# Feed-forward of two layers: the last 42 values and 42 gates share one column tile of the first matrix

## What is computed

```python
HID = int(DIM * 4 * 2 / 3)              # 682
h = shift_token(x)
mu, var = h.mean(-1, keepdims=True), h.var(-1, keepdims=True)
h = (h - mu) / jnp.sqrt(var + 1e-05) * lg + lb
h = h @ w1 + b1                         # w1: 256 x (2 * 682)
a, g = jnp.split(h, 2, axis=-1)         # values, gates
h = a * jax.nn.gelu(g, approximate=False)
x = x + h @ w2 + b2                     # w2: 682 x 256
```

## Time and profile before

| | us |
|---|---|
| median of 3 runs | 1662.73 (1662.56 to 1663.0) |
| the profiled execution | 1665.16 |
| its span in the profile | 1663.2 |
| PE busy in it | 1511.5 (91%), 9076 matmuls |
| DVE busy | 1050.4 (63%) |
| ACT busy | 903.7 (54%) |
| POOL busy | 496.5 (30%) |
| mean granted clock of PE | 0.966 |

### The profile page before, as it was taken

How to read it: one execution, slowest core, us unless ns; L and a number is a source line. 1 busy time by engine, 2 the same in 40 slices (tenths; PEclk the granted TensorE clock), 3 DMA queues, 4 the chain that set the end, 5 groups by cost and what they waited for, 6 DMA issues and landing times. The chain is left out here.

```text
span 1663.2 us, 24878 instructions
## 1 busy us (share of the span) xinstructions
PE 1511.5 (91%) x9076; PEld 988.6 (59%) x9076; DVE 1050.4 (63%) x1915; ACT 903.7 (54%) x1870; POOL 496.5 (30%) x299
## 2 busy tenths in 40 slices
PE   7889999999977999999997689997799689997898
PEld 3432222222234888887874467776577477776676
DVE  3768888888637556464555355555777455555786
ACT  5147777777742434343432487876433477776342
POOL 7100000000015100000002487775312487775113
PEclk9899999999989999999998899999799799999899
DMA  8721212200000330303005200001100100000010
GB/s 244 138 39 20 35 26 39 39 1 1 1 24 2 127 102 5 109 0 114 0 0 174 70 1 1 1 1 49 28 1 0 58 1 2 1 1 26 1 50 25
DMA packets 59312, 64.84 MB, mean 39 GB/s; under 512 B 15091, under 2 KB 48579, under 8 KB 59221
## 3 DMA queue, kind: packets, MB, share of 16 engines
q1 hardware_dynamic: 57860, 60.24, 14.3%
q10 hardware_dynamic: 1360, 3.41, 0.6%
HBM read 52.95 MB, written 10.49 MB: 38 GB/s over the span
## 5 line engine op out<-in xcount | busy, mean ns | idle before, releaser
L577 DVE TENSOR_REDUCE mcol<-bank 128x1 f32<-128x1024 f32 x256 | 302.1, 1217 | 58.5 <-PE bank L568 58.4
L662 ACT ACTIVATE a_pt<-bank 128x512 f32<-128x512 f32 x512 | 266.4, 603 | 89.0 <-PE bank L694 88.9
L694 PE MATMUL bank<-qa,ka 99*128 99x512 bf16 x512 | 193.8, 386 | 7.6 <-ACT a_pt L662 3.8
L568 PE MATMUL bank<-ka,qa 96*128 96x512 bf16 x512 | 193.7, 386 | 5.6 <-DMA ka<-k_parts 2.1
L1639 DVE CUSTOM_DVE_ANT_0 w_sm<-bank,mask 128x256 f32<-128x256 f32 (+1 forms) x256 | 89.0, 404 | 147.5 <-PE bank L1473 147.5
L1831 PE MATMUL bank<-m_hn,m_w 128*128 128x512 f32 x576 | 150.9, 419 | 19.0 <-DVE m_hn L1962 16.4
L1436 PE MATMUL bank<-wqkv,w_hst 128*128 128x512 f32 x576 | 156.4, 420 | 12.5 <-DVE w_sinp L1616 7.6
L694 PEld LDWEIGHTS bank<-qa,ka 99*128 99x128 bf16 x512 | 49.2, 98 | 165.7 <-ACT a_pt L662 121.3
L1831 PEld LDWEIGHTS bank<-m_hn,m_w 128*128 128x128 f32 x576 | 112.4, 196 | 56.0 <-issue 27.2
L705 PE MATMUL bank<-a_pt,vst 128*32 128x512 f32 x1024 | 136.4, 605 | 0.1
L1564 ACT ACTIVATE w_sm<-w_sm,w_st 128x256 f32<-128x256 f32 (+1 forms) x256 | 124.0, 489 | 19.2 <-DVE w_st L1639 19.0
(11 more groups left out here) (231 smaller groups left out, 2766.6 us busy)
## 6 DMA issues: line engine op xcount, KB each, us to landing
f_wex<-in_W SPq DMA_DIRECT2D x8, 2048.0 KB, 12.0
qa<-q_parts SPq DMA_DIRECT2D x48, 128.0 KB, 4.5
ka<-k_parts SPq DMA_DIRECT2D x48, 128.0 KB, 4.7
q_parts<-p_parts SPq DMA_DIRECT2D x16, 192.0 KB, 3.3
k_parts<-p_parts SPq DMA_DIRECT2D x8, 384.0 KB, 3.4
wqkv_raw<-in_wqkv SPq DMA_DIRECT2D x2, 1536.0 KB, 8.8
w<-in_w SPq DMA_DIRECT2D x2, 1536.0 KB, 6.4
phi<-in_phi SPq DMA_DIRECT2D x5, 512.0 KB, 3.6
```

The costliest lines, as they stand in the source:

```text
L568: last = nc.tensor.matmul(max_bank(G, r)[:, jh * HALF:(jh + 1) * HALF], G["qa"][k][0:KS, hg % 2, h, it * P:(it + 1) * P], G["ka"][k][0:KS, ...
L577: nc.vector.reduce_max(G["mcol"][hg % 2][:, p:p + 1], max_bank(G, r)[:, :], X).then_inc(G["max_free"], 1)
L662: nc.scalar.activation(pt[n % 2][:, q, :], sbank(HG * step + q), ACT.Exp, scale=HD0 ** -0.5).then_inc(p_ready, 1)
L694: mm(sbank(i), ka[k][:, q, n * P:(n + 1) * P], qa[k][:, ih, q, :], start=True, stop=True).then_inc(st_ps, 1)
```

## The change

The sixth tile of the first matrix holds both rests in one tile of 128 columns: the 42 values in columns 0 to 63, the 42 gates in columns 64 to 127. The matrix is therefore 5 x 128 values, 5 x 128 gates, and this one tile, `W1C` = 1408 columns instead of 1536. The matmuls of tile 5 leave values in rows 0 to 63 and gates in rows 64 to 127 of the bank's lower half; ACT reads the gates from the upper rows and writes gelu to rows 0 to 63; DVE works on rows 0 to 63; the second product contracts over these 64 rows. `g_ps` and `a_ps` become one semaphore `h_ps`, which counts 11 groups per half. The core of the diff:

```diff
+WHOLE = HID // P
+REST = 64
+W1C = 2 * WHOLE * P + P
...
         def w1_tile(w, f):
-            return w[:, :, :].rearrange("p k (c n) -> p k c n", c=2)[:, :, :, f * P:(f + 1) * P]
+            if f == WHOLE:
+                return w[:, :, 2 * WHOLE * P:W1C]
+            return w[:, :, 0:2 * WHOLE * P].rearrange("p k (c n) -> p k c n", c=2)[:, :, :, f * P:(f + 1) * P]
+
+        def gate_rows(f):
+
+            return slice(REST, P) if f == WHOLE else slice(0, P)
+
+        def value_rows(f):
+            return slice(0, REST) if f == WHOLE else slice(0, P)
+
+        def value_bank(f):
+            return PB[2 + f % 2][:, 0:HALF] if f == WHOLE else PB[2 + f % 2][:, HALF:2 * HALF]
...
-                            for part, (col, ready) in enumerate(((HIDP, g_ps), (0, a_ps))):
+                            cols = (WHOLE * P + f * P, f * P) if f < WHOLE else (2 * WHOLE * P,)
+                            for part, col in enumerate(cols):
...
-                                                  w1s[cw][:, k, col + f * P:col + (f + 1) * P], hns[ch][:, hf, k, :],
+                                                  w1s[cw][:, k, col:col + P], hns[ch][:, hf, k, :],
                                                   start=(n == k == 0), stop=(n == len(PRODUCTS) - 1 and k == KD - 1))
-                                last.then_inc(ready, 1)
+                                last.then_inc(h_ps, 1)
...
-                                        last = mm(PB[0][:, m * HALF:(m + 1) * HALF], w2s[cw][:, f, m * P:(m + 1) * P],
-                                                  hids[ch][:, f, :], start=(f == n == 0),
+                                        last = mm(PB[0][:, m * HALF:(m + 1) * HALF], w2s[cw][value_rows(f), f, m * P:(m + 1) * P],
+                                                  hids[ch][value_rows(f), f, :], start=(f == n == 0),
...
-                            act.wait_ge(g_ps, u + 1)
+                            act.wait_ge(h_ps, HTILES * (NH * b + hf) + min(2 * f + 1, HTILES))
                             act.wait_ge(hid_done, u - 1 if f or hf else u)
-                            S(gl[:, f % 2, :], PB[2 + f % 2][:, 0:HALF], ACT.Gelu, bias=b1[:, FT + f:FT + f + 1]).then_inc(gl_done, 1)
+                            S(gl[value_rows(f), f % 2, :], PB[2 + f % 2][gate_rows(f), 0:HALF], ACT.Gelu,
+                              bias=b1[gate_rows(f), FT + f:FT + f + 1]).then_inc(gl_done, 1)
...
                             dve.wait_ge(gl_done, u + 1)
-                            dve.wait_ge(a_ps, u + 1)
+                            dve.wait_ge(h_ps, HTILES * (NH * b + hf) + min(2 * f + 2, HTILES))
```

## The result

The changed kernel is slower, by less than half a per cent. In the first comparison its median is 1669.68 us (8 runs) against 1663.01 us of the kernel before (8 runs), ratio 1.0033, 95% interval [1.0023, 1.0044]; in a second comparison 1669.61 against 1663.14 us, ratio 1.0046 [1.0033, 1.0059]. The profiled execution took 1667.27 us at a span of 1665.3 us. The forecast was 1667.9 us, slower by 5.2 us. The ratios say 5.5 and 7.6 us, the medians 6.7 and 6.5. All ratios are those of fast runs, which leaves out one execution of e4_before_64_rows alone, at 3016.03 us.

The account below looks back on a forecast made before the run. PE was taken to bound the feed-forward halves without a gap. Late table load +2.4 us and 64-row changes +2.8 us gave +5.2 us on the 1662.73 us median: 1667.9 us, range 1661.9 to 1669.8 us.

Parts of the forecast that it names:

- Six matmuls fewer per half: Tile 5 of the first product: 1.40 us less PE work per half, 11.2 us in all, if PE needn't wait.
- The gelu table load moves behind a wait: ACT at tile 4: table load follows the gate, delaying the second product; +0.30 us per half, 2.4 us.
- Matmuls over 64 rows: Tile 5 in the second product: 14 changes between 128 and 64 rows at 0.20 us each, 2.8 us.
- Rival 1: Second product: no price for 64 rows, only the table load acts; 1665.1 us; 14%.
- rival 4: Second product: 64-row loads don't overlap with the matmul ahead; 8.0 us more, 1675.9 us; 5%.
- The table loads at the heads of the loop bodies: Head of both loop bodies: load starts with the gate, DVE 0.6 us late; taken as nothing, 1.4 us cover.
- everything else: Tile 5 on DVE and ACT, POOL's L1782, split before each loop: taken as nothing, 0.7 us left to the range.
- The sum: Whole kernel: +2.4 + 2.8 = +5.2 us, giving 1667.9 us.
- Rival 2: ACT at tile 4: table load isn't late, as ACT passes the wait sooner; -0.6 us, 1662.1 us; 7%.
- Rival 3: Second product: PE doesn't wait for tile 4's low part, gains 4.2 us until POOL's L1782 stops it; 1658.5 us; 7%.
- Rival 5: PE's new 1.4 us pause lowers the clock: +2.8 us per half, +22 us, 1690 us; 3%.
- What would show it: Timeline signs: later table load and tile 4 product, eight 1.4 us waits, load idles near 0.3 us, period 27.6 us.

Follow-up runs that it names:

- e4_before_64_rows: Kernel before, with the second product of tile 5 contracting rows 0 to 63 only, rest of the contraction left out; 1668.36 us, ratio 1.0031.
- e2_full_rows: Changed kernel, with the second product of tile 5 contracting all 128 rows again, upper 64 zeroed by GpSimd once per layer; 1664.31 us, ratio 1.0008.
- e5_before_lone_wait: Kernel before, with gates and values on one semaphore, so ACT's gate wait stands alone; all 12 matmuls of tile 5 stay; 1664.83 us, ratio 1.0011.
- e3_both: Changed kernel with ACT's two gelu waits in the other order and full 128 rows for tile 5's second product; 1658.72 us, ratio 0.9976 to the kernel before.
- e6_three_groups: e3_both with the second product in three groups: tiles 0 to 3, then 4, then 5; 1657.21 us, ratio 0.9966 to the kernel before.
- e1_wait_order: Changed kernel, with ACT waiting for hid_done first and h_ps last before the gelu; 1662.68 us, ratio 0.9997 to the kernel before.
- e8_input_earlier: e6_three_groups with both reciprocals after tile 3 and ACT instead of DVE rounding the normalised input's high part; 1649.87 us, ratio 0.9922 to the kernel before.
- e11_before_repeat: The kernel before run once more with nothing changed; 1662.63 us, ratio 0.9995.

## Why the prediction held, point by point

*Six matmuls fewer per half.* Right in both parts: 11.2 us less work on PE, 11.2 us of new wait. e2_full_rows (18 matmuls in tiles 4 and 5 of the first product) and e5_before_lone_wait (24) settle it with equal periods, 27.17 and 27.16. A wait of 1.40 in the view holds PE up by more than that: six matmuls fewer would give 26.89 - 1.40 = 25.49, e2_full_rows has 27.17, 1.68 more. The view counts from the end of the last matmul, 0.395 behind its start where the next one would start after 0.233, and after the pause the first matmul comes 0.11 behind its load: 0.16 + 0.11 = 0.27 on top of the 1.40. That is why 11.2 us less work and 11.2 us of wait leave a loss.

*The gelu table load moves behind a wait.* The step on which the sign rested, and it held. Forecast against the timeline after: table load 0.8 us after the root's end, 0.76 measured; lone wait 0.12 on DVE, 0.12 measured (1565.76 to 1565.88); gelu's product to the end of the low part 1.94, 1.93 measured (1565.88 to 1567.81); on to PE's load 0.05, 0.06 measured. From the first product to the second the load came +0.40 us later; the forecast was 1568.22 - 1567.80 = 0.42. That the first matmul follows its load by 0.11 after a pause instead of 0.23 holds too: from load to the last matmul's end it is 8.87 now, before 0.23 + 8.56 = 8.79, and 8.79 - 0.12 + 0.20 = 8.87, the 0.20 being the change to 64 rows inside it. The term of 0.30 per half measured 0.28 (e2_full_rows against the kernel before). Its lower bound, the table load not moved, was -0.43; e3_both gives -0.48.

*Matmuls over 64 rows.* 0.20 us per change was taken from a run of six L1436 matmuls in the attention stage; 0.185 came out against the changed kernel, 0.19 in the kernel before. The upper bound, the whole idle of 0.37 in the row, isn't the price: from border to border the loads lie 1.60 us apart, 0.20 over six matmuls. Rival 1 falls by the same rows; rival 4 too, since the six loads of 64 rows lie as close as those of 128 (1.23 us for six, as in the earlier trace rows). The Trainium skill (TensorEngine Tiling (Array Packing), Key Properties) says that a change of the tiling mode drains TensorE and a change of the tile alone doesn't. The trace agrees in that the loads pause 0.37 us at each change of the row height and not between the six loads of 64 rows.

*The table loads at the heads of the loop bodies, and everything else at nothing.* The waits of PE for the first layer's and the loops' products are those of before (16.4, 10.8, 3.5 and 2.6 us in total in both kernels), and POOL's L1798 ends at 1573.24 + 2.74 = 1575.98, ahead of the load at 1576.67. Right.

*The sum.* Period 27.6 forecast, 27.54 measured. Over the halves, 8 x 0.65 less the two changes that nothing follows makes 4.8 us. The ratios give 5.5 [3.8 to 7.3] and 7.6 [5.5 to 9.8]. The term that fell short is, as far as the runs show, that of the row heights: sized 2.8 us and 2.6 to 2.7 us in the halves, it is 5.2 us [3.2 to 7.2] in the whole time of e4_before_64_rows, and 1664.31 (e2_full_rows) against 1669.61 is 5.3. The prediction's upper bound of this term was 5.0, for another reason (the whole idle as the price), and the upper end of the range, 1669.8, lay 0.1 us above the result. So the mechanism and the period held, but that the median stayed inside the range is in part luck: the step priced a change only by what it does inside its stage. Some 2.5 us come on top, in the run with the first layer's changes, by a way that stays open.

*The rivals.* Rival 2 falls by the table load's row. Rival 3 isn't what happened, but its next in line, POOL, was named rightly (e6_three_groups). Rival 5, the clock: PE's pauses of 1.4 us had no price: the granted clock of the half after them is 1.00.

*What would show it.* All five signs were there: the table load; DVE's product of tile 4, 4.16 us behind the start of the first product's run (1565.88 - 1561.72) where it was 3.45 (1565.50 - 1562.05); the eight waits; the two idles (0.37 where near 0.3 was named); the period.

## What to carry to other kernels

Count the waits in front of an instruction, and look at which of them is attached and which stands alone: a table load goes with the instruction but behind the lone waits, so the wait that ends last should be the attached one; two exchanged lines were worth 0.74 us per half here, 6.9 us in the median. A saving on the busiest engine is worth only what the next arrival allows, so lay out the arrivals at every point where that engine meets the others before counting it; here a third of 1.40 us arrived once the two losses were undone, and the rest only after two further edits. A group of matmuls with fewer rows among full ones costs at both of its borders (0.19 us each here); zeroed rows avoid that.

## What the runs showed that I had not expected

- In e4_before_64_rows the short tile costs more than the halves show: 14 changes of row height, 2.7 us in the halves and 5.2 us in the median, the difference in the first layer (4.0 us against 1.5). Whether it is a price of such a tile is open. e1_wait_order has the same 14 changes, and while its halves say 8 x (26.80 - 26.89) less 2 x 0.19 = -1.1 us against the kernel before, its ratio says -0.5 [-2.5 to 1.5]: an excess of 0.6, with an interval that just reaches the 2.5 us. And e8_input_earlier, which has no short tile, gains 13.0 us [11.0 to 15.1] by its ratio where its halves give 8 x 1.37 = 11.0. Over the runs the mean granted clock was 0.964 with 64-row groups in both layers (0.9637 over six runs of e4_before_64_rows, 0.9641 and 0.9635 in the two series of the changed kernel) and 0.966 in the kernel before; 0.9637 with them in the first layer alone, 0.9652 in the second alone; with the other wait order (e1_wait_order) it was 0.9653 in spite of them. 0.002 of 1665 us are 3.3 us, an estimate from these means. That fits the excess and doesn't explain it.
- Where PE has been waiting, the same work takes different times. The 18 matmuls of L1436 (L1439 in the changed kernel) behind the first layer's stage last between 4.43 and 7.2 us, by the granted clock in them. For the second of the two runs, which follows a pause of about 3 us, it is 1.00 (the upper level, 2.4 GHz) at 4.43 us in e11_before_repeat, 0.71 at 5.97 us in the kernel before, and 0.57 at 7.20 us in e4_before_64_rows, there 0.50 (the lower level, 1.2 GHz) for the first 4.8 us; the two runs together took 11.95 and 10.40 us in two executions of the kernel before, 11.74 and 12.88 in two of the changed one, 8.87 in e2_full_rows and 14.33 in e4_before_64_rows. Such stretches differ by as much as the effect under study. The Trainium skill (TensorE: Matmul & The Clock Gate, Part 1) says that the number of slow matmuls of one kernel varies from run to run; the traces agree. The period of this stage repeats to some hundredths of a microsecond, with a granted clock of 1.00 in it, and is the better measure for what happens inside it, though, as the first point says, not for all.
